# A fused attention and expert block on one core: the token sums get a PSUM bank of their own, and the steps share three banks in turn

## The reference, cut to what matters

```python
q, k, v = heads(x, Wq, bq), heads(x, Wk, bk), heads(x, Wv, bv)      # 16 heads of 16
qp = relu(q @ rw) + 1e-6                                            # 64 features a head
kp = relu(k @ rw) + 1e-6
kv = einsum('bhsf,bhsd->bhfd', kp, v)                               # a sum over the 2048 tokens of a batch
out = (qp @ kv) / ((qp . kp.sum(tokens))[..., None] + 1e-6)
x = layernorm(x + out @ Wo + bo)
# FFN: a gated MLP and a product-key layer of 1024 experts (4 heads, best 8 of 64 x 64 sums)
mlp  = (silu(x @ Wg + bg) * (x @ Wu + bu)) @ Wd + bd
w    = silu(x @ down_embed[idx].T) * softmax(best scores)
x = layernorm(x + mlp + w @ up_embed[idx])
```

## Time and profile before

| what | value |
|---|---|
| median of 3 runs | 3934.55 us (3933.38 to 3939.51) |
| the profiled execution | 3923.38 us |
| its span, first to last instruction | 3921.6 us |
| PE busy | 3713.6 us, 95% of the span |
| PE weight loads | 3096.9 us, 79% |
| DVE busy | 3070.1 us, 78% |
| POOL busy | 1678.7 us, 43% |
| ACT busy | 1351.5 us, 34% |
| mean granted clock of PE | 0.975 of full |

### The profile page before, as it was taken

How to read it: one execution, slowest core, us unless ns; L and a number is a source line. 1 busy time by engine, 2 the same in 40 slices (tenths; PEclk the granted TensorE clock), 3 DMA queues, 4 the chain that set the end, 5 groups by cost and what they waited for, 6 DMA issues and landing times.

```text
span 3921.6 us, 50872 instructions
## 1 busy us (share of the span) xinstructions
PE 3713.6 (95%) x19388; PEld 3096.9 (79%) x19388; DVE 3070.1 (78%) x5947; ACT 1351.5 (34%) x1990; POOL 1678.7 (43%) x1004
## 2 busy tenths in 40 slices
PE   8878999999999999999999999999999999989888
PEld 7757888888888888888888888888888888777776
DVE  2277888888888888888888888887888887888883
ACT  4223333333333333333333333333334333233221
POOL 0044444354444444444444454444444444454441
PEclk9768999999999999999999999999999999999999
DMA  3000000000000000000000000000000000000000
GB/s 109 11 11 6 17 17 11 15 14 12 17 17 17 12 12 17 12 17 17 17 12 12 16 13 17 17 12 12 17 12 17 17 12 6 12 11 12 6 6 11
DMA packets 23332, 61.07 MB, mean 16 GB/s; under 512 B 5552, under 2 KB 10032, under 8 KB 23088
## 3 DMA queue, kind: packets, MB, share of 16 engines
q1 hardware_dynamic: 18480, 41.04, 3.4%
q0 software_dynamic: 4608, 16.78, 1.0%
HBM read 41.04 MB, written 16.78 MB: 15 GB/s over the span
## 4 chain that ended last, share of the span: by engine, by line
PE 77%; DVE 12%; POOL 5%; issue 5%; ACT 1%; SPq 0%; DMA 0%; DVEq 0%; POOLq 0%; ACTq 0%
PE ring L535 22%; PE y_bank L619 10%; PE y_bank L621 9%; PE kv_bank L507 5%; PE at_bank L558 5%; PE rt_bank L535 4%; DVE grid L943 4%; PE at_bank L478 3%; PE kv_bank L502 3%; PE kv_bank L478 3%; PE at_bank L549 2%; PE at_bank L464 2%; POOL grid L377 2%; DVE prob L958 2%; PE pt_bank L599 2%
## 5 line engine op out<-in xcount | busy, mean ns | idle before, releaser
L377 POOL TENSOR_TENSOR grid<-ex 128x1024 f32<-128x1024 f32 x512 | 1242.8, 2434 | 520.5 <-ACT ex L741 197.3
L943 DVE SCALAR_TENSOR_TENSOR grid<-grid,best 128x1024 f32<-128x1024 f32 x512 | 725.4, 1417 | 31.5 <-POOL grid L377 30.6
L958 DVE SCALAR_TENSOR_TENSOR prob<-grid,rz,prob 128x1024 f32<-128x1024 f32 x384 | 698.2, 1818 | 3.5
L619 PE MATMUL y_bank<-wd_sb,gate 128*128 128x256 f32 x2048 | 623.2, 386 | 12.6 <-DVE wexp L980 12.6
L621 PE MATMUL y_bank<-up_sb,wexp 128*128 128x256 f32 x2048 | 612.0, 381 | 0.0
L368 POOL TENSOR_SCALAR qp<-qp 128x512 f32<-128x512 f32 x256 | 222.7, 870 | 563.1 <-ACT qp L732 549.7
L621 PEld LDWEIGHTS y_bank<-up_sb,wexp 128*128 128x128 f32 x2048 | 390.6, 191 | 53.4
L535 PE MATMUL ring<-x1T_hl,downT_hl 128*128 128x512 f32 x1536 | 417.8, 408 | 11.1 <-ACT gate L746 11.1
L535 PE MATMUL ring<-x1T_hl,wg_hl 128*128 128x512 f32 x1536 | 423.2, 411 | 2.1 <-DVE gate L974 1.9
L535 PE MATMUL ring<-x1T_hl,wu_hl 128*128 128x512 f32 x1536 | 420.3, 409 | 0.0
L619 PEld LDWEIGHTS y_bank<-wd_sb,gate 128*128 128x128 f32 x2048 | 355.2, 191 | 55.1 <-issue 26.9
(11 more groups left out here) (122 smaller groups left out, 5754.4 us busy)
## 6 DMA issues: line engine op xcount, KB each, us to landing
xb<-in_L_attn_x SPq DMA_DIRECT2D x34, 512.0 KB, 3.6
out_y<-x POOLq DMA_DIRECT2D x32, 512.0 KB, 3.0
xa<-in_L_attn_x SPq DMA_DIRECT2D x30, 512.0 KB, 3.5
prob<-in_L_ffn_down_embed SPq DMA_DIRECT2D x1, 1024.0 KB, 5.5
prob<-in_L_ffn_Wg SPq DMA_DIRECT2D x1, 1024.0 KB, 8.3
prob<-in_L_ffn_Wu SPq DMA_DIRECT2D x1, 1024.0 KB, 10.5
wd_sb<-in_L_ffn_Wd SPq DMA_DIRECT2D x1, 1024.0 KB, 11.3
up_sb<-in_L_ffn_up_embed SPq DMA_DIRECT2D x1, 1024.0 KB, 12.2
```

Of the source, the lines that this page charges most:

```text
L377: pool.tensor_tensor(grid[:, h % 2], bcast(ex[:, h, 0:NX].unsqueeze(2), [P, NX, NK]), bcast(ex[:, RH + h, 0:NK].unsqueeze(1), [P, NX, NK]) ...
L619: pe.matmul(rows, gate[:, c % 2, t * P:(t + 1) * P], wd_sb[:, c, :], start=(c == 0 and t % 2 == 0), stop=False, skip_group_check=True)
L943: marks["keep", h] = rt_steps.mark(dve.scalar_tensor_tensor(out=g, in0=g, scalar=best[:, h, TOP - 1:TOP], in1=g, op0=ALU.is_ge, op1=ALU.mult))
L958: ins = dve.scalar_tensor_tensor(out=row, in0=g, scalar=rz[:, h:h + 1], in1=row, op0=ALU.mult, op1=ALU.add, accum_out=mass[:, 0:1] if h == ...
```

## The change

The token sums no longer share `kv_bank`. `sum_bank` holds them, and PE adds into it through all sixteen tiles of a batch: only the first matmul of a batch starts anew, only the last one signals (`summed_up`). The four additions on DVE in each body are gone; `batch_end` waits for `summed_up` and forms `kv_blocks` as the sum of the bank and a `kv_sum` that is never written again, so it no longer clears it.

The other three banks, formerly at, rt and pt together with kv, become `step_bank` 0 to 2. All uses of kv, at, rt and pt take them in turn, in the order in which PE comes to them; in the fill there are five, with the two `y_bank`. Every use waits until the use three before it (five in the fill) has been read, by a pair of semaphores for each bank. What a use needs of data is now waited for on its own: `k` and `v` for turn1, `kp` for its `k`, and so on.

```diff
+        def take(*use):
+            if use[0] == "kv" and use[2] == "sum":
+                return
+            banks = STEP_BANKS + 2 if use[0] == "kv" and use[1] < 2 * FILL else STEP_BANKS
+            k = len(place) % banks
+            place[use] = k, taken[k]
+            taken[k] += 1
+        for r in range(FILL):
+            for use in KV_SEQ:
+                for k in range(2):
+                    take("kv", 2 * r + k, *use)
+        for it in range(BG, NG + LAST_LAG):
+            kv, at, rt, ff = (0 <= it - lag < NG for lag in (0, ATTN_LAG, ROUTE_LAG, FFN_LAG))
+            for c in range(C):
+                for name, group, uses in (("kv", it, KV_FIRST[c] if kv else []),
+                                          ("at", it - ATTN_LAG, AT_EARLY[c] if at else []),
+                                          ("rt", it - ROUTE_LAG, [(c // 2,)] if rt and c % 2 == 0 else []),
+                                          ("kv", it, KV_EARLY[c] if kv else []),
+                                          ("at", it - ATTN_LAG, AT_MID[c] if at else []),
+                                          ("pt", it - FFN_LAG, [(c,)] if ff else []),
+                                          ("kv", it, KV_LATE[c] if kv else []),
+                                          ("at", it - ATTN_LAG, AT_LATE[c] if at else [])):
+                    for use in uses:
+                        take(name, group, *use)
+        def free(eng, *use):
+            k, nth = place[use]
+            if nth:
+                eng.wait_ge(bank_read[k], nth)
...
+            def add_up(a, t):
+                lane, i = in_lane(a)
+                first, last = a % BG == t == 0, (a + 1) % BG == 0 and t == T - 1
+                pe.wait_ge(*drained("kv", a, "v", t // 2))
+                pe.wait_ge(*drained("kv", a, "kp", 2 * t + 1))
+                if first:
+                    wait(pe, blocks_ready, a // BG)
+                for c in range(FC):
+                    mm = pe.matmul(sum_bank[:, c * VW:(c + 1) * VW], lane.kp[:, c * P:(c + 1) * P],
+                                   lane.v[:, t % 2, c, :], start=(first and c == 0), stop=False,
+                                   skip_group_check=True)
...
+                    if last:
+                        mm.then_inc(summed_up, 1)
...
                 elif kind == "k":
+                    pe.wait_ge(*drained("kv", a, "turn", 1))
                     mm = project(bank, wk_sb, lane.xT, j)
                 elif kind == "kp":
+                    pe.wait_ge(*drained("kv", a, "k", half))
...
                 def rt_use(t):
                     if t == 0:
-                        pe.wait_ge(at_read, (s + 1) * AT_USES)
-                    wait(pe, rt_read, s * T + t)
+                        pe.wait_ge(*drained("at", s, "next", 0))
+                        pe.wait_ge(*drained("at", s, "next", 1))
+                    free(pe, "rt", s, t)
...
                 def ff_weights(c):
-                    wait(pe, wexp_ready, n * C + c)
                     if c == 0:
                         pe.wait_ge(prob_ready, (n + 1) * T)
+                    free(pe, "pt", n, c)
...
             def batch_end(b):
-                dve.wait_ge(kv_read, in_main((b + 1) * BG) * KV_USES)
+                dve.wait_ge(summed_up, b + 1)
...
-                    dve.tensor_copy(kv_blocks[rows, :, g2, 0:DK], kv_sum[rows, :, g2 * DK:(g2 + 1) * DK])
+                    dve.tensor_tensor(kv_blocks[rows, :, g2, 0:DK], sums[rows, :, g2 * DK:(g2 + 1) * DK],
+                                      kv_sum[rows, :, g2 * DK:(g2 + 1) * DK], ALU.add)
...
-                clear_sum()
```

More of the change, by code:

```diff
@@ L64, in block_kernel @@
     KV_USES, AT_USES = len(KV_SEQ), len(AT_SEQ)
[L65 to L66 removed]
+    STEP_BANKS, FILL = 3, BG // 2
     x_groups = x.rearrange("b s d -> (b s) d").rearrange("(g p t) d -> g p t d", p=P, t=T)
@@ L238, in fill_lanes @@
                 for k, (kind, j) in enumerate(KV_SEQ):
-                    for lane in LANES:
-                        use(lane, r, kind, j)
+                    for a in (2 * r, 2 * r + 1):
+                        use(a, kind, j)
                     if r == FILL - 1 and k < PREP_STEPS:
@@ L481, in project_rows, with kv_use @@
                 return mm
-            def kv_use(lane, i, kind, j):
-                bank = lane.bank
-                wait(pe, lane.read, i * KV_USES + KV_U[kind, j])
+            def add_up(a, t):
+                lane, i = in_lane(a)
+                first, last = a % BG == t == 0, (a + 1) % BG == 0 and t == T - 1
[7 more added lines that the diff above has]
+                                   skip_group_check=True)
+                if t == T - 1:
+                    pe.wait_ge(lane.summed, i + 1)
+                    sums = sum_bank[:, 0:FC * VW].rearrange("p (c w) -> p c w", c=FC)[:, :, 0:2 * DK]
+                    for k in range(KD):
+                        mm = pe.matmul(sums, lane.xs[:, k:k + 1].broadcast_to([P, P]), wv_sb[:, k, :],
+                                       start=False, stop=(last and k == KD - 1), skip_group_check=True)
+                    if last:
+                        mm.then_inc(summed_up, 1)
+            def kv_use(a, kind, j):
+                lane, i = in_lane(a)
+                if kind == "sum":
+                    add_up(a, j)
+                    return
+                bank = bank_of("kv", a, kind, j)
+                free(pe, "kv", a, kind, j)
                 if kind == "turn":
@@ L816, in prep, with lows @@
                     low(wu_hl[:, 1], wu_rows, wu_hl[:, 0], low_ready)
-            def lows(blocks, half, bank, bias, high, group, s):
+            def lows(blocks, half, bank, bias, high, group):
                 for i in range(2):
@@ L826, in lows, with kv_use @@
                                                    op0=ALU.add, op1=ALU.subtract)
-                ins.then_inc(s, 1)
+                return ins
             def pair(bank):
                 return bank[:].rearrange("p (t d) -> p t d", t=2)
-            def kv_use(lane, i, kind, j, batch=0):
+            def kv_use(a, kind, j):
+                lane, i = in_lane(a)
+                if kind not in ("k", "v"):
+                    return
+                bank = bank_of("kv", a, kind, j)
                 if kind == "k":
-                    lows(lane.k_hl, j, lane.bank, bk_sb, lane.high, i, lane.read)
+                    read_by(lows(lane.k_hl, j, bank, bk_sb, lane.high, i), "kv", a, kind, j)
@@ L953, in add_head @@
                         if t == 0:
-                            wait(dve, pt_full, (s - 1) * C)
+                            if s >= 2:
+                                dve.wait_ge(*full("pt", s - 2, C - 1))
                         ins = dve.tensor_scalar(row, g, rz[:, 0:1], None, ALU.mult)
@@ L1002, in uses @@
                         if use[0] in ("k", "v", "sum") and kv:
-                            kv_use(main, in_main(a), *use, batch=batch)
+                            kv_use(a, *use)
                         if use[0] in ("q", "qkv", "wo", "next") and at:
```

219 lines of the change are left out of this document (115 added, 104 removed).

## The result

The changed kernel takes 3955.38 us (median of 6 runs, 3951.25 to 3962.18), the kernel before, run beside it, 3926.26 (6 runs, 3916.39 to 3939.51). The ratio is 1.0075, 95% interval 1.0049 to 1.0102. The profiled execution took 3953.06 us, with a span of 3951.3 against 3921.6 before: 29.7 more. The forecast was 3948: 13 us more than the 3934.55 that the kernel before had shown in its first three runs. So the direction and the time came out, but the difference is 29 us in the medians and 29.7 in the profile, more than twice the 13.

What follows compares the result with a forecast made beforehand. PE's list of work was taken as the bound, with 2.6 us idle a body. 60 us more in full bodies less 47 at the ends made 3936.5, plus 11.2 for the median: 3948 us, range 3905 to 3980.

Steps and rivals of the forecast that it cites:

- pt0 behind rt0: Full bodies, c = 0: pt0 waits until DVE has read rt0 and starts 1.63 us later, 31.0 us over 19 bodies.
- pt2 behind rt1: Full bodies, c = 2: pt2 waits for the late reading of rt1, 0.61 us a body, 15.9 us in 26 bodies.
- Does k1 swallow it?: Full bodies, c = 1: forecast no; rival said idle time at q1 and k1 covers pt0's wait, giving 3904 us; chance 13%.
- the wait at k1 would be shorter: Sign expected in the profile after: k1's wait still there, shorter by what q1 no longer waits, pt1 taking some.
- Batch bodies: A batch's first body: pt0's wait lengthened by the batch end on DVE, 2.25 us each, 13.5 us for six.
- The clock in c = 1: Rival: clock falls in full bodies after the new waits, 1.6 us in each of 25, 40 us, 3988 us; chance 13%.
- The repeating gap: PE's two waits, 1.7 us before k1 and 0.9 before q1, repeat alike in each full body.
- no bubbles: Rival, full bodies: both old waits go and nothing new comes, 67 us less there, 3820 us in all; chance 4%.
- The start: Fill, body 4 and body 5: idle time of PE goes, saving 5, 14 and 8 us.
- regained clock: Rival, body 4: PE's work returns from clock 0.72 to full clock, 16 us less, 3932 us; chance 12%.
- The end: Bodies 32 to 35: waits of qp0, qp4 and qp6 go, q0 starts 1.15 later; 4.9 us sooner each, 20 in all.
- DVE's additions and the new semaphore waits: Full bodies: four additions of 0.43 us and about 31 new PE waits a body, both taken at nothing.

Runs made afterwards that it cites:

- the last experiment: Changed kernel, six uses of c = 1 and 2 on other banks than in turn, DVE reading tile 0's scores before the last stage's rows: 3837.56 us, ratio 0.9757.
- the scores first: Changed kernel, DVE doing the scores of tile 0 ahead of the last stage's rows in c = 0: 3886.94 us, ratio 0.989 to the kernel before.
- Without turns: Changed kernel, sums keeping their bank, kv and at one bank each, rt and pt sharing the third: ratio 1.0146 to the kernel before.
- the kernel before with the two waits: Kernel before, with even pt transposes (pt0, pt2, pt4, pt6) made to wait until their part's rt was read: ratio 1.022, plain full body 117.70 us.
- the exponential first: Changed kernel, ACT doing the exponential of tile 0's scores ahead of the highs of q0: ratio 1.0104 to the kernel before, plain full body 119.0 us.
- the kernel before with the scores first: Kernel before, only DVE's order changed, tile 0's scores ahead of the last stage's rows: ratio 1.0025, plain full body 115.54 to 115.6 us.

## Why the prediction was right, and where its sizes were off

The direction and the mechanism were right; that the time came within 7.4 us of 3955.38 is partly luck. The profiled execution was forecast at 3936.5 and took 3953.06, 16.6 more. To this the forecast added 11.2 for the median, as before; the median after lies only 2.3 above its execution. Most of the 16.6 is one thing that the sum took at nothing and left to rivals, a change of the clock: it cost about 27 us in the full bodies and 4 at the end, and gave back 12 at the start.

**pt0 behind rt0**: right. 1.63 was forecast for a plain body, 1.62 measured in the changed kernel and 1.64 with this wait alone. **pt2 behind rt1**: the wait is there, 0.57 in body 13 (0.66 forecast for that pair), but it adds only where PE comes on time: 9.0 instead of 15.9.

**Does k1 swallow it?** No, as argued: the lows of k0 end 1.62 later, counted from the gate product, and PE loses at pt1 (0.68) and k1 what it won at q1. The last paragraph of the prediction turned this around when it said that the wait at k1 would be shorter. It grew, from 1.66 to 2.17: PE stands before k1 only 1.11 later, since q1 no longer holds it for 0.93, while the reader is 1.62 later. Time that PE wins ahead of a fixed reader lengthens the wait.

**Batch bodies**: the term was mis-sized, 22.1 instead of 13.5. The wait is close (2.54 against 2.25; the body in which the clock held grew by 2.4), but the forecast gave it no lower clock; behind it the granted clock fell to 0.50 in five of six, and these lost another 1.5 or more, some 8 us in all.

**The clock in c = 1**: the step that failed in size. The forecast took full bodies at a clock of 1.00 and gave 13% to a fall after the new waits. Besides the five batch bodies the fall came in 12 bodies and cost 19.3 us; with the batch bodies that makes 27, two thirds of the rival's 40. The 12 are in another place than the rival had it: not at the waits that were new, but on k1's product behind the grown wait of 2.17. The prediction named a clock that left 1.00 as a sign that it was wrong, and bodies 14 and 16 have 0.99. Behind a wait the granted clock falls to 0.50 in the 12 bodies (k1's product takes 3.60 us against 1.98 in body 14) and in the five batch bodies, and not in the other nine.

**The repeating gap**, which spoke for "no bubbles": by the last experiment the gaps were a matter of banks, but not of too few of them: with the same three, other pairs and the scores first, PE's idle time went from 5.2 to 1.5 us in body 13. My "no bubbles" at 3820 lay near what the kernel can do, not near what turns do.

**The start**: body 4 gained 26.1 instead of 14. The idle time fell from 17.0 to 3.1, which is the 14; the other 12 is PE's own work, 60.75 us before and 48.46 after, as the granted clock rose from 0.72 to 0.87. That is the rival *regained clock*, at 12 of its 16 us. Without turns neither came (76.6 us, 0.72). Body 5 was as forecast; the fill's 3.9 looks like the forecast 5 but is within what the fill varies by.

**The end**: 12.9 instead of 20. Bodies 33 and 35 gained 4.9 and 5.0, exactly the term, with the new wait at q0 behind rt0 (1.7 us); bodies 32 and 34 gained 1.1 and 2.0. Both have a clock of 0.95, 33 and 35 have 0.98. The difference lies in c = 7, 21 us instead of 19: behind the waits for the last `wexp` and for the reader of x, the output products stay at a granted clock of 0.50 for 6.8 us, to the end of the body, as here in body 34 (3668.95 to 3675.70); in bodies 33 and 35 it is 3.3 us.

```profile
3667.60 0.67 PE L700 MATMUL y_bank<-wd_sb,gate 128*128 128x256 f32 x2 [2.49 <-DVE wexp L1061]
...
3671.14 1.09 PE L520 MATMUL step_bank<-ident_r,x 128*128 128x128 f32 x4 [1.01 <-DVE x L988]
3672.02 1.06 PE L700 MATMUL y_bank<-wd_sb,gate 128*128 128x256 f32 x2
```

**DVE's additions and the new semaphore waits**: nothing in full bodies. The first is shown by the kernel that puts the additions back. For the second, a plain body takes 117.7 us in the kernel before with the two waits, without the new semaphores, and 117.7 in the kernel without turns, with them; no run shows the up to 16 us that the forecast's range allowed the semaphores. DVE is busy 70 us less, more than the 55 forecast; the additions are 55 of them.

## What to carry to other kernels

When banks are handed out in turn, write down for each use which one lies exactly that many places before it and when its last reader is done; here the pair that was late by 1.57 us cost 1.62 us in every plain body. Here turns helped where the engines wait for one another unevenly (body 4, 26 us, 12 of them by the clock) and hurt where the order of the reader was made for fixed banks. Count the waits that you lengthen, too: here, behind waits of 1.9 to 2.5 us, the granted clock fell to 0.50 in 17 of 26 bodies, which no sum of waits contains. Then move the reader first (the scores ahead of the rows) and choose the pairs by hand in the parts that bind, following PE to the next late reader each time: here that turned 0.75% slower into 2.4% faster.

## What the runs showed that I had not expected

A wait of the same length was followed by a slow product in some bodies and not in others, and the counts differ with what came before. In the changed kernel k1's product, behind 2.17 us of idle time (1.92 in four bodies), ran slowly (2.67 to 3.68 us) in 12 of the 20 bodies that had a wait at pt0 (1.77, once 2.54) some 16 us ahead of it and came through that at a granted clock of 1.00. It ran slowly in none of the five where the clock had fallen to 0.50 at pt0 already, and not in body 6, which has no wait there. With the additions back on DVE it was 15 of 23 and none of two. With the scores first, so without the wait at pt0, it was 1 of 26. In the full bodies of the three kernels in which the wait was 1.66 behind one of 1.6 at pt0, it took 1.98 every time. What in the history decides isn't settled.

The other surprise is the normalisation on DVE that took 1.99 us instead of 0.41 beside POOL's pass over the grid. It stands in each of the bodies 7 to 31 with the exponential first, and in three full bodies of the kernel before with the scores first, just the three that are 1.6 us longer. The kernel before and the changed one have no such case. Where it took so long, the normalisation starts 0.06 to 0.19 us behind the start of POOL's pass; in the kernel before and the changed one those that meet such a pass start 0.23 ahead of it and take 0.41. So here work that was brought forward met another engine's at a worse moment, at 1.6 us each time.
